# A fused convolution, attention and expert block: the first batch's side work dealt out anew over VectorE, GpSimd and TensorE

## The chip, the core and the metric

The kernel runs on one core of a Trainium2 chip. The metric is the device time in microseconds of one execution. All arrays are float32; the whole input, four images of 96 channels and 56 x 56 pixels, is worked through in one launch.

## The reference

What is computed, cut to what matters (x is (4, 96, 56, 56)):

```
xn    = layernorm over channels of x                       # eps 1e-6
value = depthwise 3x3 conv(xn, w_v) + b_v                  # stride 1
query = depthwise 3x3 conv(xn, w_q) + b_q                  # stride 1
key   = depthwise 3x3 conv(xn, w_k) + b_k                  # stride 2, 28 x 28
off   = depthwise 3x3 conv(xn, w_off1) + b_off1            # stride 2, 28 x 28
o     = gelu(layernorm over channels of off * ln_g + ln_b)
pos   = tanh(o @ w_off2 + reference points)                # (y, x) of each of 784 samples
vs    = bilinear sample of value at pos                    # four rows of value a sample
attn  = (query^T key) * 32^-0.5                            # 12 heads, 32 channels; no softmax
x     = x + w_out @ (attn vs)
t     = layernorm over channels of x, a row a pixel
gates = softmax(t @ gate_w + gate_b), the best 2 of 4 kept and renormalised
out   = x + sum over 4 experts of gate * (gelu(t @ w1 + b1) @ w2 + b2)
```

As there is no softmax in the attention, the kernel forms key times sampled values first, folds w_out into it, and applies the result to the query.

## The kernel before

Each engine runs its own instruction list in order; semaphores join them. The work goes batch by batch. The experts' matmuls of a batch (84 chunks of 448 pixels and 128 hidden units) are laid between the attention steps of the next batch by tables of numbers, which the change does not touch. The first batch has no experts to be laid between, so its attention part stands alone in roughly the first 140 us. Only this part changes.

The three functions head, first_rest and those that they call, on each engine, are the first batch:

- The image arrives in three DMAs. TensorE turns it into rows of pixels in seven slots, ScalarE evicts them, VectorE takes the statistics (L1098, then small instructions L1075 to L1088). The scaling is shared: VectorE scales the first tiles (L1114), ScalarE the last ones (L846). TensorE turns the image back into 128 partitions (a quarter of the image's rows by 32 channels, three blocks), and ScalarE writes it into a padded image xpad (L873), on which all four convolutions work. TensorE runs idle matmuls (spin, L607) where it would stand.
- The value and query convolutions of blocks 0 and 1 run on TensorE as nine accumulating matmuls with diagonal weights on half a block (convolve, L580); the diagonals are built by GpSimd (L1503). Block 2 of each, and the offset and key convolutions (stride 2, three blocks) run on VectorE, nine taps a block (tap, L1146 and L1149).
- offc: the normalised offsets are transposed on TensorE, ScalarE applies gelu (L896), TensorE multiplies by w_off2 (offsets, L601), VectorE adds the reference points (raw_positions, L1188), ScalarE applies tanh (L900), VectorE works out row numbers and weights (positions, to L1214).
- The values are transposed to rows of pixels in seven slots (valT, L631, L925), and SP writes them to a table in memory by four DMAs (L480): two after the fourth slot, two after the seventh. GpSimd gathers from the table by the row numbers, 16 indirect DMAs, two a tile (L1485), after both the row numbers and all four writes are there. VectorE weights them (sample, L1351 and L1354).
- key_values (L642), the head mask (L1364) and mixes (L652) follow, then attended (L672), the products with the query.

The PSUM tiles pa and pd are each used in turn by a list of jobs (act_jobs for ScalarE's evictions, dve_jobs for VectorE's); a job waits for the one two places ahead of it. The float32 expert weights are split into a high and a low part before the experts: w1 lies in the query's memory until then, so nothing may be written to query before weights_split. Names: KEYS_AHEAD key taps stand ahead of the positions; VALUE_HALF is the slot at which the first two table writes are issued; py, ph are PSUM tiles of TensorE's products.

## Time and profile before

| | us |
|---|---|
| median of 3 runs (748.31 to 748.81) | 748.49 |
| the profiled execution | 748.6 |
| its span, from the first instruction to the last | 746.8 |
| TensorE busy | 715.4 (96%) |
| VectorE busy | 583.9 (78%) |
| ScalarE busy | 384.6 (51%) |
| GpSimd busy | 213.0 (29%) |

Busy time is a sum over the whole span, and a busy TensorE is not TensorE at its peak: a float32 matmul has two records, and the granted clock (0.978 of 2.4 GHz in the mean) enters their length. For a change at one place the start and end of single instructions there say more. In the rows below a line's first number is the start in us from the span's start, the second the length in us; "x24" is the number of instructions merged; a bracket gives how long the engine stood before it and what ended that.

### The profile page before, as it was taken

The page shows a single profiled execution, that of the slowest core. Times are in us where ns is not written, and L with a number is a line of the kernel's source. Part 1 is how long each engine was busy: PE and PEld are TensorE (multiplying, and loading weights), DVE is VectorE, ACT ScalarE, POOL GpSimd, SP SyncE. Part 2 cuts the span into 40 slices and gives each one's busy share as a digit, 9 for nine tenths or more (in the row PEclk, how much of TensorE's full clock was granted, in tenths as well). Part 3 has the DMA queues.
Part 4 walks back from the last instruction along what each step waited for, and adds up shares of the span by engine and source line. Part 5 has one row for each costly group of instructions (what it writes and reads, how often), then busy time and mean ns, then how long its engine had stood idle before and what let it go on. Part 6 is the DMA issues. An engine that isn't in the chain of part 4 may idle for free.

```text
span 746.8 us, 9679 instructions
## 1 busy us (share of the span) xinstructions
PE 715.4 (96%) x3216; PEld 495.4 (66%) x3216; DVE 583.9 (78%) x1512; ACT 384.6 (51%) x722; POOL 213.0 (29%) x184
## 2 busy tenths in 40 slices
PE   7898999999999999899999999999989999999996
PEld 5556666566676666566766665666656665888884
DVE  6889558999999768799998577999955275677774
ACT  2313124754554525644646238545423256899995
POOL 4002700012138500111177101211375121344443
PEclk9798999999999999999999999999989999999998
DMA  8007200134464411354744403444545201121111
GB/s 199 6 0 203 57 1 1 40 74 92 95 187 114 107 30 14 73 128 93 195 105 113 70 11 58 83 102 91 165 103 111 32 28 41 47 74 47 66 47 37
DMA packets 29697, 58.66 MB, mean 79 GB/s; under 512 B 6224, under 2 KB 20176, under 8 KB 29360
## 3 DMA queue, kind: packets, MB, share of 16 engines
q0 software_dynamic: 11584, 17.90, 15.4%
q1 hardware_dynamic: 14336, 32.59, 14.3%
q10 hardware_dynamic: 3728, 7.55, 3.2%
q8 instruction: 26, 0.43, 0.3%
q14 instruction: 23, 0.19, 0.1%
HBM read 30.30 MB, written 14.65 MB: 60 GB/s over the span
## 4 chain that ended last, share of the span: by engine, by line
PE 81%; ACT 5%; DMA 4%; DVE 4%; POOL 2%; issue 2%; POOLq 0%; ACTq 0%; DVEq 0%
PE py L759 20%; PE pd L672 8%; PE ph L580 7%; PE ph L775 5%; PE ph L776 5%; PE ph L777 5%; PE pa L531 3%; PE pa L660 3%; PE pd L642 2%; PE ph L797 2%; PE ph L799 2%; PE ph L798 2%; PE py L809 2%; PE py L812 2%; PE py L810 2%
## 5 line engine op out<-in xcount | busy, mean ns | idle before, releaser
L759 PE MATMUL py<-hid,w 128*96 128x448 f32 x504 | 233.6, 544 | 8.0 <-ACT hid L1021 7.2
L1021 ACT ACTIVATE hid<-ph,b 128x448 f32<-128x448 f32 x252 | 158.9, 632 | 150.8 <-PE ph L777 147.3
L775 PE MATMUL ph<-x_hi,w_hi 96*128 96x448 f32 x252 | 164.6, 653 | 0.0
L1496 POOL DMA_DIRECT2D xbuf<-ye x76 | 64.3, 846 | 331.0 <-DMA xbuf<-ye 159.7
L1485 POOL DMA_INDIRECT big<-value_table,rows x64 | 86.2, 1348 | 88.3 <-DVE rows L1209 54.4
L759 PEld LDWEIGHTS py<-hid,w 128*96 128x96 f32 x504 | 81.3, 164 | 27.7 <-ACT hid L1021 11.8
L776 PE MATMUL ph<-x_lo,w_hi 96*128 96x448 f32 x252 | 93.2, 370 | 0.0
L777 PE MATMUL ph<-x_hi,w_lo 96*128 96x448 f32 x252 | 92.4, 367 | 0.0
L1432 DVE SCALAR_TENSOR_TENSOR ye<-py,b,gate_all 96x448 f32<-96x448 f32 x112 | 75.3, 675 | 11.5 <-PE py L759 7.9
L1498 POOL TENSOR_TENSOR xbuf<-xbuf,ye 96x448 f32<-96x448 f32 x36 | 53.9, 1498 | 102.5 <-DVE ye L1432 99.8
L1459 DVE TENSOR_TENSOR hid_lo<-hid,hid_hi 128x448 fp32r<-128x448 f32 x84 | 59.7, 711 | 27.2 <-ACT hid L1030 27.0
L1149 DVE SCALAR_TENSOR_TENSOR query<-xpad,conv_w,query 128x784 f32<-128x784 f32 x80 | 78.3, 1027 | 0.5
L1149 DVE SCALAR_TENSOR_TENSOR val<-xpad,conv_w,val 128x784 f32<-128x784 f32 x80 | 78.3, 1026 | 0.4
L775 PEld LDWEIGHTS ph<-x_hi,w_hi 96*128 96x128 f32 x252 | 48.0, 190 | 41.1 <-issue 40.7
L776 PEld LDWEIGHTS ph<-x_lo,w_hi 96*128 96x128 f32 x252 | 48.7, 193 | 35.9 <-issue 35.5
L672 PE MATMUL pd<-query,mix_area 128*96 128x392 f32 x192 | 67.2, 492 | 0.0
L1030 ACT ACTIVATE hid_hi<-ph,b 128x448 fp32r<-128x448 f32 x84 | 53.3, 634 | 6.9 <-PE ph L799 1.7
L1030 ACT ACTIVATE hid<-ph,b 128x448 f32<-128x448 f32 x84 | 52.5, 625 | 0.0
L841 ACT ACTIVATE big<-pa 112x400 f32<-112x400 f32 x28 | 14.0, 502 | 70.6 <-PE pa L660 70.6
L777 PEld LDWEIGHTS ph<-x_hi,w_lo 96*128 96x128 f32 x252 | 47.8, 190 | 3.5
L672 PEld LDWEIGHTS pd<-query,mix_area 128*96 128x96 f32 x192 | 29.5, 163 | 24.0 <-issue 24.0
L1370 DVE TENSOR_TENSOR xbuf<-pd,xbuf 96x392 f32<-96x392 f32 x32 | 17.9, 561 | 32.7 <-PE pd L672 32.5
(168 smaller groups left out, 1092.2 us busy)
## 6 DMA issues: line engine op xcount, KB each, us to landing
gate_all<-gate_rows SPq DMA_DIRECT2D x56, 336.0 KB, 3.4
xbuf<-ye POOLq DMA_DIRECT2D x76, 168.0 KB, 3.5
value_table<-valT ACTq DMA_DIRECT2D x6, 1176.0 KB, 8.5
out<-xbuf SPq DMA_DIRECT2D x28, 168.0 KB, 2.0
xbuf<-in_x SPq DMA_DIRECT2D x3, 1176.0 KB, 10.6
value_table<-valT SPq DMA_DIRECT2D x2, 672.0 KB, 5.4
big<-value_table,rows POOLq DMA_INDIRECT x64, 2.8
value_table<-valT SPq DMA_DIRECT2D x2, 504.0 KB, 5.0
```

The costliest lines, as they stand in the source:

```text
L672: last = nc.tensor.matmul(bank[0:C, 0:YPIX], mix[:, q, i, :], query[:, i, h * YPIX:(h + 1) * YPIX], start=(i == 0), stop=(i == BLOCKS - 1))
L759: nc.tensor.matmul(py[e % 2][0:C, 0:GPIX], w2[:, c, :], hid[:, k % 3, :], start=(j == 0), stop=(j == CPE - 1)).then_inc(hid_used, 1)
L775: nc.tensor.matmul(bank, w1_hi[:, cols], xh(b, g), start=True, stop=False)
L776: nc.tensor.matmul(bank, w1_hi[:, cols], xl(b, g), start=False, stop=False)
L777: nc.tensor.matmul(bank, w1_lo[:, cols], xh(b, g), start=False, stop=True).then_inc(hid_full, 1)
L1021: nc.scalar.activation(hid[:, k % 3, :], ph[k % 2][:, 0:GPIX], ACT.Gelu, bias=b1[:, k % NCH:k % NCH + 1]).then_inc(hid_act, 1)
L1030: nc.scalar.activation(dst[:, k % 3, :], ph[k % 2][:, 0:GPIX], ACT.Gelu, bias=b1[:, k % NCH:k % NCH + 1]).then_inc(ready, 1)
L1149: ins = v.scalar_tensor_tensor(to, src, w, to, ALU.mult, ALU.add)
L1432: v.scalar_tensor_tensor(ye[0:C, e, :], py[e % 2][0:C, 0:GPIX], b2[:, e:e + 1], gate_all[0:C, e, :], ALU.add, ALU.mult).then_inc(ye_ready, 1)
L1459: v.tensor_tensor(hid_lo[:, m % 2, :], hid[:, k % 3, :], hid_hi[:, k % 3, :].bitcast(f32), ALU.subtract).then_inc(hid_lo_ready, 1)
L1485: p.indirect_dma_start(got[:, tile, r, :, :].rearrange("p a c -> p (a c)"), None, table, bass.IndirectOffsetOnAxis(ap=rows[:, r, tile:tile ...
L1496: pool.dma_start(to, ye[0:C, e, :], accum_op=ALU.add).then_inc(ye_summed, 16)
```

## The change

All of it concerns the first batch.

- GpSimd, idle between the diagonals and the gathers, gets the upper half (392 of 784 elements a partition) of value block 2: one tensor_scalar, then eight times a tensor_scalar into a scratch half and a tensor_tensor that adds it. Behind it come the splits of w1 and w2, which stood on VectorE ahead of the offset taps. TensorE waits for the half block (value_low) ahead of the value transposes.
- VectorE does the lower half of value block 2 (half_tap, nine taps of 392), and takes over one of TensorE's eight half-block convolutions, the lower half of query block 1, in nine such taps behind the keys. Each tap waits for the one before.
- The offset norm and its transposes and gelu come ahead of all value transposes; the offset products stand behind four value slots (seven before), the tanh on ScalarE behind six. Three key taps instead of nine stand ahead of the raw positions, one more ahead of the tanh's result, five behind.
- TensorE transposes the offset tiles behind its second value convolution instead of its third. The gate-mean product moves between the first two, with the wait for the constants.
- VectorE scales five tiles instead of four and ScalarE two slots instead of three. TensorE spins twice instead of three times at the start and eight times instead of five behind the first transposes.

TensorE's list from the first convolution to the key-value products, before. L580 are convolutions, nine matmuls each; L568 transposes of offset (kv_area) and key tiles; L631 value slots, three matmuls each; L513 the transposes of normalised offsets; L601 the offset products; L531 the second batch's slots.

```order
16 L580 MATMUL ph<-xpad,xbuf 128x392 x27
17 L568 MATMUL pa<-ident,kv_area 98x128 x6
18 L580 MATMUL ph<-xpad,xbuf 128x392 x9
19 L623 MATMUL py<-gate_w,hid 96x4
20 L631 MATMUL pa<-ident,val 112x128 x12
21 L513 MATMUL pa<-ident,kv_area 96x98 x8
22 L631 MATMUL pa<-ident,val 112x128 x9
23 L601 MATMUL pd<-woff,mix_area 98x2 x8
24 L531 MATMUL pa<-ident_gate,xbuf 112x96 x8
25 L580 MATMUL ph<-xpad,gate_all 128x392 x18
26 L568 MATMUL pa<-ident,key_area 98x128 x6
27 L580 MATMUL ph<-xpad,ye 128x392 x18
```

The same place of TensorE's list now; the lines are L596, L584, L651, L529, L619 and L547 in the changed file.

```order
16 L596 MATMUL ph<-xpad,xbuf 128x392 x9
17 L639 MATMUL py<-gate_w,hid 96x4
18 L596 MATMUL ph<-xpad,xbuf 128x392 x9
19 L584 MATMUL pa<-ident,kv_area 98x128 x6
20 L596 MATMUL ph<-xpad,xbuf 128x392 x18
21 L529 MATMUL pa<-ident,kv_area 96x98 x8
22 L651 MATMUL pa<-ident,val 112x128 x12
23 L619 MATMUL pd<-woff,mix_area 98x2 x8
24 L651 MATMUL pa<-ident,val 112x128 x9
25 L547 MATMUL pa<-ident_gate,xbuf 112x96 x8
26 L596 MATMUL ph<-xpad,gate_all 128x392 x18
27 L584 MATMUL pa<-ident,key_area 98x128 x6
```

The offset transposes, which wait for the offset taps, now have two convolutions ahead of them and two behind. The transposes of the normalised offsets are ahead of every value slot, and the last query convolution is one instead of two.

VectorE's list from the scaling to the norm, before. kv_area holds the offsets, val the values.

```order
26 L1114 TENSOR_TENSOR xT<-xT,rstd 112x384 x3
27 L1227 CAST w_hi<-query 96x1536
28 L1228 TENSOR_TENSOR w_lo<-query,w_hi 96x1536
29 L1449 CAST w_hi<-w 128x1152
30 L1451 TENSOR_TENSOR w_lo<-w,w_hi 128x1152
31 L1146 TENSOR_SCALAR kv_area<-xpad,conv_w,conv_b 128x196 x3
32 L1149 SCALAR_TENSOR_TENSOR kv_area<-xpad,conv_w,kv_area 128x196 x24
33 L1146 TENSOR_SCALAR val<-xpad,conv_w,conv_b 128x784
34 L1149 SCALAR_TENSOR_TENSOR val<-xpad,conv_w,val 128x784 x8
35 L1176 BN_STATS st<-kv_area 98x6 x8
```

The same place of VectorE's list now.

```order
26 L1135 TENSOR_TENSOR xT<-xT,rstd 112x384 x4
27 L1167 TENSOR_SCALAR kv_area<-xpad,conv_w,conv_b 128x196 x3
28 L1170 SCALAR_TENSOR_TENSOR kv_area<-xpad,conv_w,kv_area 128x196 x24
29 L1185 TENSOR_SCALAR val<-xpad,conv_w,conv_b 128x392
30 L1188 SCALAR_TENSOR_TENSOR val<-xpad,conv_w,val 128x392 x8
31 L1213 BN_STATS st<-kv_area 98x6 x8
```

The four instructions of the splits are gone from it and the value taps have half their width.

The diff, without the declarations of the new semaphores and without three places where the numbers of scaled tiles are written as functions of the batch (scaled_by_dve and slots_scaled: FIRST_SCALED tiles in the first batch, TOP_TILES + 1 = 4 in the others):

```diff
--- before
+++ after
@@ -68,7 +68,7 @@
 
 def act_jobs():
 
-    order = jobs(0, "xT", NG) + jobs(0, "pad", 2 * BLOCKS) + jobs(0, "offT", 2) + jobs(0, "valT", QT)[:VALUE_HALF] + jobs(0, "offc", 2) + jobs(0, "valT", QT)[VALUE_HALF:]
+    order = jobs(0, "xT", NG) + jobs(0, "pad", 2 * BLOCKS) + jobs(0, "offT", 2) + jobs(0, "offc", 2) + jobs(0, "valT", QT)
     order += jobs(1, "xT", NG)[:EARLY_SLOTS] + jobs(0, "keyT", 2) + jobs(1, "xT", NG)[EARLY_SLOTS:] + jobs(0, "mix", QUARTERS) + jobs(0, "x1T", NG) + jobs(1, "pad", 2 * BLOCKS)
     order += jobs(0, "gateT", 1) + jobs(1, "offT", 2) + jobs(1, "offc", 2)
     for b in range(1, BATCH):
...
@@ -111,7 +111,10 @@
 
 QUERY_AHEAD = 2
 VALUE_AHEAD = 2
-KEYS_AHEAD = 9
+KEYS_AHEAD, KEYS_TO_TANH = 3, 4
+HALF = QH // 2
+FIRST_SCALED = 5
+OFFSETS_BEHIND, LIMIT_BEHIND = 4, 6
 SCALE_AFTER = 4
 FIRST_SPLITS, GATES_AFTER = 2, 3
 
...
@@ -398,7 +414,7 @@
             return dve_job(b, name, g)[1]
 
 
-        first_convs = [(m, i, h) for m in (VALUE, QUERY) for i in range(2) for h in range(2)]
+        first_convs = [(VALUE, 0, 0), (VALUE, 0, 1), (VALUE, 1, 0), (VALUE, 1, 1), (QUERY, 0, 0), (QUERY, 0, 1), (QUERY, 1, 0)]
         VALUE_CONVS = 4
 
         def dve_blocks(b):
...
@@ -608,19 +626,21 @@
 
             def head(b):
                 pe.wait_ge(zeros_ready, 1)
-                spin(3)
+                spin(2)
                 pe.wait_ge(tiles_zero, 1)
                 x_to_tokens(b)
-                spin(5)
+                spin(8)
                 quarters_back(b)
                 pe.wait_ge(act_done, acted(b, "pad", 2 * BLOCKS - 1))
                 pe.wait_ge(diag_ready, 2)
-                convolve(3)
+                pe.wait_ge(consts_in, NCONST)
+                pe.wait_ge(mean_filled, 1)
+                convolve(1)
+                nc.tensor.matmul(py[0][0:C, 0:EXPERTS], mean_of, gate_w[:, :], start=True, stop=True).then_inc(gate_mean, 1)
+                convolve(1)
                 to_samples(b, "offT", off, off_conv, 1)
-                convolve(1)
-                pe.wait_ge(mean_filled, 1)
-                pe.wait_ge(consts_in, NCONST)
-                nc.tensor.matmul(py[0][0:C, 0:EXPERTS], mean_of, gate_w[:, :], start=True, stop=True).then_inc(gate_mean, 1)
+                convolve(2)
+                off_to_channels(b)
 
             def values_to_tokens(b, before=lambda s: None, slots=range(QT)):
                 for s in slots:
...
@@ -706,19 +726,20 @@
 
             def first_rest(b, plan, chunks_to):
                 pe.wait_ge(conv_done, VALUE_CONVS)
-                values_to_tokens(b, slots=range(VALUE_HALF))
-                off_to_channels(b)
-                values_to_tokens(b, slots=range(VALUE_HALF, QT))
+                pe.wait_ge(value_low, 1)
+                values_to_tokens(b, slots=range(OFFSETS_BEHIND))
                 offsets(b)
+                values_to_tokens(b, slots=range(OFFSETS_BEHIND, QT))
                 x_to_tokens(b + 1, slots=range(EARLY_SLOTS))
                 pe.wait_ge(diag_ready, 4)
                 convolve(2)
                 to_samples(b, "keyT", key, key_conv, b + 1)
-                convolve(2)
+                convolve(1)
                 x_to_tokens(b + 1, slots=range(EARLY_SLOTS, QT))
                 key_values(b, range(QUARTERS))
                 mixes(b)
                 pe.wait_ge(conv_done, len(first_convs))
+                pe.wait_ge(query_low, 1)
                 pe.wait_ge(gate_centred, 1)
                 attended(b)
                 quarters_back(b + 1)
...
@@ -913,9 +934,11 @@
                 scaled(b)
                 padded(b)
                 act.wait_ge(conv_in, 32)
-                convolved(0, 3)
+                convolved(0, 2)
                 off_to_samples(b)
-                convolved(3, 4)
+                convolved(2, 4)
+                act.wait_ge(consts_in, NCONST)
+                off_gelu(b)
 
             def values_to_tokens(b, before=lambda s: None, slots=range(QT)):
                 for s in slots:
...
@@ -965,16 +988,14 @@
                 limit_positions(b)
 
             def first_rest(b, plan, gelus_to):
-                values_to_tokens(b, slots=range(VALUE_HALF))
-                act.wait_ge(consts_in, NCONST)
-                off_gelu(b)
-                values_to_tokens(b, slots=range(VALUE_HALF, QT))
+                values_to_tokens(b, slots=range(LIMIT_BEHIND))
                 limit_positions(b)
+                values_to_tokens(b, slots=range(LIMIT_BEHIND, QT))
                 x_to_tokens(b + 1, slots=range(EARLY_SLOTS))
                 act.wait_ge(weights_split, 1)
                 convolved(4, 6)
                 key_to_samples(b)
-                convolved(6, 8)
+                convolved(6, 7)
                 x_to_tokens(b + 1, slots=range(EARLY_SLOTS, QT))
                 mixes(b)
                 act.wait_ge(dve_done, dved(b, "kv", QUARTERS - 1))
...
@@ -1109,10 +1130,10 @@
 
             def scale_x(b):
                 by = x_stats_of(b).rstd[0:TP, :].rearrange("p (s o j u) -> p s o j u", j=QUARTERS, o=1, u=1)
-                for s in range(TOP_TILES + 1):
+                for s in range(scaled_by_dve(b)):
                     part = tiles_of(s)
                     ins = v.tensor_tensor(part, part, by[:, s, :, :, :].to_broadcast([TP, BLOCKS, QUARTERS, CB]), ALU.mult)
-                    if s >= TOP_TILES - 1:
+                    if s in (TOP_TILES - 1, scaled_by_dve(b) - 1):
                         ins.then_inc(x_normed, 1)
 
             def norm_x(b, turn):
...
@@ -1154,6 +1175,22 @@
 
             tapped = {}
 
+            def half_tap(m, i, k, dst, ready):
+
+                dy, dx = k // 3 + HALF, k % 3
+                src = xpad[:, i, dy:dy + HALF, dx:dx + W]
+                to = dst[:, i, HALF * W:].rearrange("c (h w) -> c h w", w=W)
+                w = conv_w[:, m, i, k:k + 1]
+                if k == 0:
+                    ins = v.tensor_scalar(to, src, w, conv_b[:, m, i:i + 1], ALU.mult, ALU.add)
+                else:
+                    need(tapped[(m, i)])
+                    ins = v.scalar_tensor_tensor(to, src, w, to, ALU.mult, ALU.add)
+                if k < TAPS - 1:
+                    tapped[(m, i)] = step(ins)
+                else:
+                    ins.then_inc(ready, 1)
+
             def off_tap(k):
                 tap(OFF, k, off, 2, off_conv, range(BLOCKS))
 
...
@@ -1223,16 +1260,12 @@
             def head(b):
 
                 norm_x(b, no_turn)
-                dve.wait_ge(consts_in, NCONST)
-                link(v.tensor_copy(w1_hi[:, :], w1))
-                v.tensor_tensor(w1_lo[:, :], w1, w1_hi[:, :].bitcast(f32), ALU.subtract).then_inc(weights_split, 1)
-                split_w2()
                 dve.wait_ge(conv_in, 32)
                 dve.wait_ge(act_done, acted(b, "pad", 2 * BLOCKS - 1))
                 for k in range(TAPS):
                     off_tap(k)
                 for k in range(TAPS):
-                    value_tap(b, k)
+                    half_tap(VALUE, 2, k, val, val_conv)
                 normalise_off(b, no_turn)
                 dve.wait_ge(gate_mean, 1)
                 v.tensor_tensor(ident_gate[:, C:XC], gate_w[:, :], py[0][0:C, 0:EXPERTS], ALU.subtract).then_inc(gate_centred, 1)
...
@@ -1241,9 +1274,14 @@
                 for k in range(KEYS_AHEAD):
                     key_tap(k)
                 raw_positions(b, no_turn)
+                for k in range(KEYS_AHEAD, KEYS_TO_TANH):
+                    key_tap(k)
                 positions(b, no_turn)
-                for k in range(KEYS_AHEAD, TAPS):
+                for k in range(KEYS_TO_TANH, TAPS):
                     key_tap(k)
+                dve.wait_ge(weights_split, 1)
+                for k in range(TAPS):
+                    half_tap(QUERY, 1, k, query, query_low)
                 for k in range(TAPS):
                     query_tap(b, k)
                 sample(b, no_turn)
...
@@ -1443,13 +1481,6 @@
 
                 return turn
 
-            def split_w2():
-
-
-                v.tensor_copy(w2_hi[:, :, :], w2[:, :, :]).then_inc(w2_part, 1)
-                dve.wait_ge(w2_part, 1)
-                v.tensor_tensor(w2_lo[:, :, :], w2[:, :, :], w2_hi[:, :, :].bitcast(f32), ALU.subtract).then_inc(w2_split, 1)
-
             def last_experts(outputs_to):
 
                 for k in range(EARLY_CHUNKS, ALL_CHUNKS):
...
@@ -1502,6 +1533,27 @@
             for m, i in ((VALUE, 0), (VALUE, 1), (QUERY, 0), (QUERY, 1)):
                 p.tensor_tensor(diag_of[(m, i)], ident[:, :].rearrange("c (o d) -> c o d", o=1).to_broadcast([128, TAPS, 128]),
                                 conv_w[:, m, i, :].rearrange("c (k o) -> c k o", o=1).to_broadcast([128, TAPS, 128]), ALU.mult).then_inc(diag_ready, 1)
+            pool.wait_ge(act_done, acted(0, "pad", 2 * BLOCKS - 1))
+            top = val[:, 2, 0:HALF * W].rearrange("c (h w) -> c h w", w=W)
+            parts = xbuf[2][:, 2 * TAPS * 128:2 * (TAPS * 128 + HALF * W)].rearrange("c (n p) -> c n p", n=2)
+            for k in range(TAPS):
+                src, w = xpad[:, 2, k // 3:k // 3 + HALF, k % 3:k % 3 + W], conv_w[:, VALUE, 2, k:k + 1]
+                if k == 0:
+                    ins = p.tensor_scalar(top, src, w, conv_b[:, VALUE, 2:3], ALU.mult, ALU.add)
+                else:
+                    part = parts[:, k % 2, :]
+                    p.tensor_scalar(part.rearrange("c (h w) -> c h w", w=W), src, w, None, ALU.mult).then_inc(value_part, 1)
+                    pool.wait_ge(value_part, k)
+                    pool.wait_ge(value_step, k)
+                    ins = p.tensor_tensor(val[:, 2, 0:HALF * W], val[:, 2, 0:HALF * W], part, ALU.add)
+                ins.then_inc(value_low if k == TAPS - 1 else value_step, 1)
+            pool.wait_ge(consts_in, NCONST)
+            p.tensor_copy(w1_hi[:, :], w1).then_inc(w1_part, 1)
+            pool.wait_ge(w1_part, 1)
+            p.tensor_tensor(w1_lo[:, :], w1, w1_hi[:, :].bitcast(f32), ALU.subtract).then_inc(weights_split, 1)
+            p.tensor_copy(w2_hi[:, :, :], w2[:, :, :]).then_inc(w2_part, 1)
+            pool.wait_ge(w2_part, 1)
+            p.tensor_tensor(w2_lo[:, :, :], w2[:, :, :], w2_hi[:, :, :].bitcast(f32), ALU.subtract).then_inc(w2_split, 1)
             pool.wait_ge(table_edge, 32)
             added = 0
             for b in range(BATCH):
```

## Rows read from the trace of the kernel before

**Rows 1.** Chain of waits, first 140 us: start, length, engine, tile, line, records
```profile
27.46 19.96 PE ph L580 x54
...
60.45 0.56 PE pa L631 x3
...
61.69 2.03 PE pd L601 x16
...
80.47 11.86 PE ph L580 x36
...
96.31 5.16 PE pd L642 x16
...
104.26 5.93 PE pd L672 x18
```

**Rows 2.** VectorE's timeline, first batch: start, length, engine, line, operation, shapes, number
```profile
28.86 8.96 DVE L1149 SCALAR_TENSOR_TENSOR kv_area<-xpad,conv_w,kv_area 128x196 f32<-128x196 f32 x24
...
38.46 8.53 DVE L1149 SCALAR_TENSOR_TENSOR val<-xpad,conv_w,val 128x784 f32<-128x784 f32 x8
48.46 1.38 DVE L1176 BATCH_NORM_STATS2 st<-kv_area 98x6 f32<-98x96 f32 x8 [1.47 <-ACT kv_area L881]
...
54.93 0.14 DVE L1238 TENSOR_TENSOR ident_gate<-gate_w,py 96x4 f32<-96x4 f32 x1
...
65.80 0.17 DVE L1198 TENSOR_SCALAR pos<-pt 98x16 f32<-98x16 f32 x1 [0.28 <-ACT pt L900]
...
68.64 0.16 DVE L1209 TENSOR_SCALAR rows<-ix 98x8 int32<-98x8 f32 x1
...
70.07 8.57 DVE L1149 SCALAR_TENSOR_TENSOR query<-xpad,conv_w,query 128x784 f32<-128x784 f32 x8
...
94.11 1.46 DVE L1354 SCALAR_TENSOR_TENSOR key_area<-big,w,key_area 98x96 f32<-98x96 f32 x6
```

**Rows 3.** GpSimd's timeline, gathers of the first batch
```profile
69.74 1.37 POOL L1485 DMA_INDIRECT big<-value_table,rows  x1 [54.45 <-DVE rows L1209]
71.41 1.64 POOL L1485 DMA_INDIRECT big<-value_table,rows  x1 [0.30 <-issue]
...
91.38 0.96 POOL L1485 DMA_INDIRECT big<-value_table,rows  x1 [0.30 <-issue]
```

**Rows 4.** Busy time by stretch: PE, PEld, DVE, ACT, POOL, clock, DMA, GB/s
```profile
22.00:31.00 9.00, 8.06 (x29) 6.30 (x30) 6.54 (x12) 2.87 (x6) 0.00 (x0) 0.50 0.01 3
```

**Rows 5.** ScalarE's timeline: gelu, last value slot, paddings of the second batch
```profile
57.78 1.28 ACT L896 ACT_TABLE_LOAD   x1 [0.36 <-PE pa L513]
59.07 1.24 ACT L896 ACTIVATE mix_area<-pa,ln_gb 96x392 f32<-96x392 f32 x2
...
61.72 0.49 ACT L925 ACTIVATE valT<-pa 112x384 f32<-112x384 f32 x1 [0.18 <-PE pa L631]
...
127.02 0.92 ACT L873 ACTIVATE xpad<-pa 128x392 f32<-128x392 f32 x2 [0.56 <-PE pa L558]
...
129.71 1.25 ACT L873 ACTIVATE xpad<-pa 128x504 f32<-128x504 f32 x2 [0.22 <-PE pa L536]
```

**Rows 6.** Timelines of GpSimd and VectorE near 14 and 610 us
```profile
13.19 2.10 POOL L1503 TENSOR_TENSOR ye<-ident,conv_w 128x1152 f32<-128x1152 f32 x1
...
14.55 0.81 DVE L1075 TENSOR_TENSOR sd<-st 112x28 f32<-112x28 f32 x1
...
604.79 1.13 POOL L1498 TENSOR_TENSOR xbuf<-xbuf,ye 96x448 f32<-96x448 f32 x1 [15.75 <-DVE ye L1432]
610.09 2.65 POOL L1498 TENSOR_TENSOR xbuf<-xbuf,ye 96x448 f32<-96x448 f32 x1 [4.17 <-DVE ye L1432]
...
611.67 1.21 DVE L1376 TENSOR_TENSOR sc<-big,rstd 112x112 f32<-112x112 f32 x1
```

**Rows 7.** Table writes of the first batch: issue and time to landing
```profile
L480 SPq DMA_DIRECT2D value_table<-valT x4: 304/406/631, 57.4 to 62.6; - x4
...
DMA to landing us min/median/max: 4.4/5.0/6.3
```

21 lines of the change are left out of this document (16 added, 5 removed).

## The prediction

> **What bounds the kernel now.** I read the chain that ended last first. In the first 140 us its long pieces are TensorE's [rows 1], so I looked for the place where the changed stretch, the first batch, hands over to the rest: the first attention products, which start at 104.26 us. Behind them the program is the same in both kernels, so whatever moves that moment moves the end by about as much.
>
> Two lines of work meet ahead of it, and the reader should follow both. One is TensorE: eight convolutions, 5.93 us each where it runs at full speed (36 records, two a matmul, in 11.86 us), then the key-value products from 96.31 [rows 1]. The other is the positions: the offset convolution on VectorE, its norm (done when VectorE goes on at 54.93), transposes, gelu, offset products, positions (row numbers at 68.8), sixteen gathers on GpSimd from 69.74 to 92.34, and sampling until 95.57 [rows 2, 3]. The two reach the key-value products within 0.8 us of each other. So taking a convolution off TensorE alone gives at most 0.8 us, and any delay of the positions beyond 0.8 us goes into the time in full. The change must be judged by when the gathers start.
>
> **The start.** ScalarE scales 8 pieces instead of 12, VectorE 5 tiles instead of 4. Eight spinning matmuls instead of 5 fill most of TensorE's pause before the padding transposes. In the kernel before the granted clock falls behind that pause: it is 0.50 (1.2 GHz) from 22 to 31 us [rows 4]. I assume that it holds now (2.4 GHz). Then the scaled image is padded at about 20.7 + 3.9 = 24.7, the 3.9 being the same six evictions of the second batch at full clock (127.02 to 130.96) [rows 5], against 27.4 before, where the first offset taps start 1.3 us ahead of 28.86 [rows 2]. The weight splits that leave VectorE cost nothing there before: they lay in its wait for the padding. Gain of this part: 2.7 us.
>
> **What VectorE does by its own durations.** Offset taps 10.2 us (3 and 24 pieces). Half a value block: nine taps of 392, between 0.37 (196 elements) and 1.07 us (784), by a straight line 0.61, so 5.6 instead of 9.2. Norm 6.5 (48.46 to 54.93) [rows 2]. Alone, the norm would end at 24.7 + 10.2 + 5.6 + 6.5 = 47.0, 8 us before its old 54.9.
>
> **What GpSimd adds, and the port.** GpSimd was idle from 15.3 to 69.7. Now it has 21 instructions from 24.7 on: 9 products of one tensor by a pointer (392 elements), 8 additions of two, two casts and two subtractions (1536 and 1152). Two-input ones have rows: 448 elements 1.13 us undisturbed, 1152 elements 2.10 [rows 6]. The straight line through them gives 1.05 for 392 and 2.63 for 1536. One-input ones have no row. They cost between nothing (if they keep nobody waiting) and the two-input price; I take 0.6, 1.6 and 1.3, a little over half of it, since they read half as much. Sum: 8 x 1.05 + 9 x 0.6 + 1.6 + 2.63 + 1.3 + 2.10 = 21.4 us; bounds 13 and 27.
>
> These do not lie beside VectorE's work, and that is the core of my forecast. At 14.55 a VectorE tensor_tensor of 28 elements, which has two inputs in SBUF, took 0.81 us, where small VectorE instructions take 0.16 or 0.17 [rows 2]; it ended 0.07 us behind the GpSimd instruction that ran from 13.19 to 15.29. At 610.09 a GpSimd addition took 2.65 us instead of 1.13: it waited for two VectorE instructions, and the next VectorE one, started at 611.67, took 1.21 and ended 0.14 us behind it [rows 6]. Each excludes the other while it runs. Every tap of VectorE (scalar_tensor_tensor: padded image and accumulator) has two inputs in SBUF.
>
> So each GpSimd instruction takes its time out of VectorE's, less what VectorE can hide of its fixed part, about 0.2 us (196 elements last 0.37, 784 last 1.07, so some 0.14 to 0.2 is not data). 21.4 - 21 x 0.2 = 17.2 us. All of it falls ahead of the end of the norm, since 17 + 22 us is longer than GpSimd's whole list. The norm ends at 47.0 + 17.2 = 64.2. Bounds: 47.0 (no exclusion) and 47.0 + 27 - 2 = 72.
>
> The Trainium skill, "SBUF — State Buffer", section "SBUF: two separate sides", calls this shared pair an exclusive lock held for the whole instruction. By full durations the loss would be 21.4 and the norm's end 68.4; that is 4 us more than my term. For the one-input products the "GPSIMD Engine Reference", section "Elementwise — side-by-side cycle accounting", has 1.03 cycles an element at most two operations; 392 elements would be an estimated 0.34 us and a dispatch, and my sum some 1 us less. No row here shows it.
>
> **TensorE in that stretch.** The offset tiles are transposed behind two convolutions now, ready at 24.7 + 11.9 = 36.6, but the offset taps end late: 17 GpSimd instructions (13.8 - 3.4 = 10.4) and the first two splits (3.8) fall among them, so 24.7 + 10.2 + 14.2 = 49. TensorE stands 12 us, with a lower clock behind it: the first three convolutions of the kernel before began at the low clock and took 19.96 instead of 17.8, so 2.2 [rows 1]. Its other two convolutions end at 49 + 0.7 + 11.9 + 2.2 = 63.8, just when the norm does.
>
> **From the norm to the gathers.** Transposes and gelu with its table load 3.1 (from the first transpose, 0.6 ahead of 57.78, to 60.31) [rows 5]; four value slots 2.2 (0.56 each on TensorE); offset products 2.0 [rows 1]; raw positions 0.4; one key tap 1.1 (three pieces of the 24 in 8.96 us), beside which the two value slots in front of the tanh are evicted (0.5 more); tanh to row numbers 3.0 (65.80 to 68.80) [rows 2]. 64.2 + 3.1 + 2.2 + 2.0 + 0.4 + 1.1 + 0.5 + 3.0 = 76.5. The last value slot follows the tanh's at about 74.2; its two table writes, issued in some 0.4 to 0.6 us each, take 5.0 more [rows 7]: 80.2. In the kernel before that landing (61.72 + 0.49 + 6 = 68.2) came ahead of the row numbers; now it is what the gathers wait for. They start at 80.2 instead of 69.7: +10.5.
>
> **To the hand-over.** Sixteen gathers take 22.6. One issued beside VectorE's query taps took up to 1.64 us, one late in the row 0.96 [rows 3]; VectorE has 20.6 us of taps beside them now (5 key, half a query block, a query block) instead of 9.3, which I put at 1.7. Last gather 104.5, sampled 3.2 later (92.34 to 95.57), 107.7. TensorE has done its three convolutions and token transposes at 98 and waits. The first two quarters of products are done; two remain, 2.6 of the 5.16 us [rows 1], behind a masking (0.6), then the mixes 2.8: 113.7. Before: 104.26. That is +9.4, and TensorE is cold after its wait, another 2.2 at most; I take 1.6. **Sum: +11.0 us** on the profiled execution's 748.6 (its span 746.8), which is 0.1 above the median of the runs, so 759.5.
>
> **Rivals.**
> *The work hides as meant* (chance 0.15). If strided taps and GpSimd products share the port, the norm ends at 47.0; TensorE's four convolutions end at 49.1; gelu at 52.3, last value slot 58, table 64, gathers 64 to 88.3, sampled 91.5, hand-over 96.9 to 99: 5 to 7 us gained, 742.5. For it: the norm really has 8 us of slack gained. Against: every two-input row that I found beside GpSimd shows the wait. It decides once the loss is under 5 us: table landing and longer tail need the norm by about 52.
> *VectorE keeps the port* (0.08). At 610.09 GpSimd was passed over once by a queued instruction. Passed over throughout the offset and value taps, it would begin its list near 41 and hold the value half block until 57. TensorE's value slots stand behind that wait and the offset products behind them; table at 68.5, hand-over 102 to 105: 746 to 749.
> *Half a loss* (0.15): 8 to 10 us instead of 17, since GpSimd waits between its own dependent steps. Then 750 to 755.
> *GpSimd at its upper price* (0.07): loss 23 to 25, about 767; if it still held its list past 80, the gathers would queue behind the splits too.
>
> **How the numbers follow.** Main case 0.55, 756 to 764. Faster by over 0.2%: 0.16 (first rival and a little of the second); within 0.2%, about what a measurement of this kernel can tell from no change: 0.05; slower: 0.79. The range leaves out most of the first rival and the far end of the last: 744 to 768; the main case alone has 754 to 765.
>
> **What would show it.** Right: the 27 offset taps take over 20 us; GpSimd additions of 1.05 us show up as 1.3 and more; the norm ends behind 60; TensorE stands before the offset transposes; the first gather waits for the table and starts behind 76. Wrong: offset taps done in 10 to 11 us and a first gather ahead of 69. If the clock falls in the padding after all, 2 us are to be added.

## The result, and the profile after

| | before | after |
|---|---|---|
| median (range, executions) | 748.4 us (746.95 to 748.81, 4) | 759.1 us (755.83 to 764.28, 4) |
| the profiled execution, its span | 748.6, 746.8 | 755.8, 754.0 |
| hand-over (first attention products) | 104.09 | 112.57 |
| TensorE, VectorE, GpSimd busy | 715.4, 583.9, 213.0 | 712.7, 594.8, 248.1 |

The changed kernel takes 1.0153 times as long (95% interval 1.0092 to 1.0214); forecast were 759.5 us and "slower". The profiled execution is the fastest of its four: in it the hand-over comes 8.5 us later and the end 7.2, against 11.0 forecast. (In the timeline the hand-over of the kernel before stands at 104.09, in the chain of rows 1 at 104.26; below I use the timeline's for all kernels.) GpSimd's busy time grew by 35 us; its 21 new instructions are 30.1 of them (24 to 76 us), and that already holds waiting. The medians below are of all executions of a kernel, while the ratios leave out those more than 1.5% above its fastest, among them e11's profiled one.

GpSimd's timeline of the changed kernel, which answers to its silence until 69.74 in [rows 3]:

```profile
24.48 0.66 POOL L1542 TENSOR_SCALAR val<-xpad,conv_w,conv_b 128x392 f32<-128x392 f32 x1 [9.57 <-ACT xpad L894]
25.13 1.27 POOL L1545 TENSOR_SCALAR xbuf<-xpad,conv_w 128x392 f32<-128x392 f32 x1
26.48 1.25 POOL L1548 TENSOR_TENSOR val<-val,xbuf 128x392 f32<-128x392 f32 x1
27.71 1.37 POOL L1545 TENSOR_SCALAR xbuf<-xpad,conv_w 128x392 f32<-128x392 f32 x1
29.16 1.11 POOL L1548 TENSOR_TENSOR val<-val,xbuf 128x392 f32<-128x392 f32 x1
...
45.58 1.79 POOL L1551 CAST w_hi<-query 96x1536 fp32r<-96x1536 f32 x1
47.46 3.63 POOL L1553 TENSOR_TENSOR w_lo<-query,w_hi 96x1536 fp32r<-96x1536 f32 x1
...
52.60 2.82 POOL L1556 TENSOR_TENSOR w_lo<-w,w_hi 128x1152 fp32r<-128x1152 f32 x1
78.42 1.21 POOL L1516 DMA_INDIRECT big<-value_table,rows  x1 [23.00 <-DMA value_table<-valT]
...
100.10 1.43 POOL L1516 DMA_INDIRECT big<-value_table,rows  x1 [0.30 <-issue]
```

Its VectorE, answering to [rows 2]. The last row is the same form as the second, later, with GpSimd only gathering:

```profile
25.76 14.81 DVE L1170 SCALAR_TENSOR_TENSOR kv_area<-xpad,conv_w,kv_area 128x196 f32<-128x196 f32 x24
...
41.20 11.73 DVE L1188 SCALAR_TENSOR_TENSOR val<-xpad,conv_w,val 128x392 f32<-128x392 f32 x8
52.86 1.36 DVE L1213 BATCH_NORM_STATS2 st<-kv_area 98x6 f32<-98x96 f32 x8
54.26 1.19 DVE L1095 TENSOR_TENSOR sa<-st 98x8 f32<-98x8 f32 x1
...
60.34 0.14 DVE L1271 TENSOR_TENSOR ident_gate<-gate_w,py 96x4 f32<-96x4 f32 x1
...
80.96 5.26 DVE L1188 SCALAR_TENSOR_TENSOR query<-xpad,conv_w,query 128x392 f32<-128x392 f32 x8
```

The offset taps take 14.81 us where they took 8.96, though nothing on VectorE changed in them. The half value block takes 11.73, and the same nine-tap form 5.26 when GpSimd computes nothing. The small addition at 54.26, 1.19 us long, ends 0.03 us behind the last subtraction on GpSimd, which ends at 55.42; the eight BATCH_NORM_STATS2 before it, which have one input, lie beside the same subtraction and take 1.36 us, as without it (1.37 in e2). The norm is done at 60.34 instead of 54.93.

One period of the offset taps, tap by tap, beside the addition at 29.16 and the product behind it:

```profile
29.32 1.17 DVE L1170 SCALAR_TENSOR_TENSOR kv_area<-xpad,conv_w,kv_area 128x196 f32<-128x196 f32 x1
30.26 1.37 POOL L1545 TENSOR_SCALAR xbuf<-xpad,conv_w 128x392 f32<-128x392 f32 x1
30.42 0.74 DVE L1170 SCALAR_TENSOR_TENSOR kv_area<-xpad,conv_w,kv_area 128x196 f32<-128x196 f32 x1
31.20 0.42 DVE L1170 SCALAR_TENSOR_TENSOR kv_area<-xpad,conv_w,kv_area 128x196 f32<-128x196 f32 x1
31.54 0.41 DVE L1170 SCALAR_TENSOR_TENSOR kv_area<-xpad,conv_w,kv_area 128x196 f32<-128x196 f32 x1
```

An undisturbed tap has 0.42 and starts 0.37 behind the last (8.96 us for 24). So the addition costs VectorE about 0.7 us and the product about 0.35, and the product itself takes 1.37 where the first one, beside a one-input tap, took 0.66: each engine waits for the other.

The chain of waits of the changed kernel, answering to [rows 1] (start, length, engine, tile, line, records):

```profile
66.62 2.50 PE pd L619 x16
...
71.44 0.50 ACT valT L948
72.30 5.12 DMA value_table<-valT
...
105.47 4.48 PE pd L662 x8
109.95 2.78 PE pa L672 x24
112.73 5.93 PE pd L692 x18
```

Before, TensorE's convolutions were the chain at 80 us. Now it runs through the norm, the offset products and value slots, the value table (72.30 to 77.42), all gathers (78.42 on) and the sampling; TensorE waits for them. The row numbers were there at 74.2, so the table's landing releases the gathers, as forecast.

Busy time by stretch of the changed kernel (start:end, length, busy time of PE, PEld, DVE, ACT and POOL, then the granted clock, DMA share, GB/s):

```profile
58.00:76.00 18.00, 13.92 (x64) 11.77 (x65) 11.37 (x50) 7.04 (x13) 0.00 (x0) 0.51 0.43 127
...
105.00:118.00 13.00, 12.53 (x49) 7.62 (x50) 5.01 (x19) 1.64 (x4) 0.00 (x0) 0.87 0.00 0
```

From 58 to 76 us, behind TensorE's waits for the offset taps and the norm, the clock stands at its lower level (0.51); the value slots and offset products lie there. From 105 to 118, behind the wait for the samples, it is 0.87.

### The profile page after: what moved, and what is told of

The parts are those of the page before. It is cut to its first block, busy times and chain, and to the rows that moved or that the text cites. A ratio compares the mean times of both kernels' runs of the same rounds, so it can differ in the third digit from the quotient of the medians.

```text
span 754.0 us, 9684 instructions
## 1 busy us (share of the span) xinstructions
PE 712.7 (95%) x3202; PEld 493.2 (65%) x3202; DVE 594.8 (79%) x1518; ACT 383.5 (51%) x717; POOL 248.1 (33%) x205
## 4 chain that ended last, share of the span: by engine, by line
PE 60%; DMA 11%; DVE 10%; POOL 8%; ACT 5%; issue 5%; POOLq 0%; ACTq 0%; SPq 0%; DVEq 0%
PE py L780 15%; PE pd L692 8%; DMA xbuf<-ye 7%; POOL big L1516 6%; PE ph L796 4%; PE ph L797 4%; PE ph L798 4%; PE pa L680 3%; DVE kv_area L1170 3%; DMA value_table<-valT 2%; PE ph L818 2%; PE ph L820 2%; PE ph L819 2%; PE py L830 2%; PE py L833 2%
## 5 line engine op out<-in xcount | busy, mean ns | idle before, releaser
L780 PE MATMUL py<-hid,w 128*96 128x448 f32 x504 | 233.2, 544 | 10.3 <-ACT hid L1042 7.1
L1527 POOL DMA_DIRECT2D xbuf<-ye x76 | 68.1, 896 | 325.4 <-DVE ye L1470 156.0
L780 PEld LDWEIGHTS py<-hid,w 128*96 128x96 f32 x504 | 81.3, 164 | 30.0 <-ACT hid L1042 11.7
L1529 POOL TENSOR_TENSOR xbuf<-xbuf,ye 96x448 f32<-96x448 f32 x36 | 53.9, 1498 | 102.4 <-DVE ye L1470 99.7
L1170 DVE SCALAR_TENSOR_TENSOR query<-xpad,conv_w,query 128x784 f32<-128x784 f32 x80 | 78.4, 1028 | 0.5
L797 PEld LDWEIGHTS ph<-x_lo,w_hi 96*128 96x128 f32 x252 | 48.4, 192 | 35.3 <-issue 34.8
L1170 DVE SCALAR_TENSOR_TENSOR val<-xpad,conv_w,val 128x784 f32<-128x784 f32 x72 | 70.0, 1025 | 0.1
L1051 ACT ACTIVATE hid<-ph,b 128x448 f32<-128x448 f32 x84 | 52.5, 625 | 0.0
## 6 DMA issues: line engine op xcount, KB each, us to landing
xbuf<-in_x SPq DMA_DIRECT2D x3, 1176.0 KB, 10.4
```

Of the source, the lines that this page charges most:

```text
L780: nc.tensor.matmul(py[e % 2][0:C, 0:GPIX], w2[:, c, :], hid[:, k % 3, :], start=(j == 0), stop=(j == CPE - 1)).then_inc(hid_used, 1)
L797: nc.tensor.matmul(bank, w1_hi[:, cols], xl(b, g), start=False, stop=False)
L1051: nc.scalar.activation(dst[:, k % 3, :], ph[k % 2][:, 0:GPIX], ACT.Gelu, bias=b1[:, k % NCH:k % NCH + 1]).then_inc(ready, 1)
L1170: ins = v.scalar_tensor_tensor(to, src, w, to, ALU.mult, ALU.add)
L1527: pool.dma_start(to, ye[0:C, e, :], accum_op=ALU.add).then_inc(ye_summed, 16)
```

## The experiments

My theory: two-input work of GpSimd and VectorE excludes each other, VectorE's list grows by GpSimd's time, and the positions chain carries that into the hand-over one for one. Rivals: GpSimd does not disturb, and the delay is in the new order of TensorE's list; or it is memory traffic in general and not the reading. Each ratio is to the kernel before on the same chip (its medians beside e1 to e12: 747.9 and 748.6). Executions start unevenly: the first offset tap (T0) comes between 24.45 and 28.84 us in kernels that have the new start (e4 aside). Two sources show in the traces. In e5 and e9 TensorE's first transposes take 10.6 us instead of 6.5; in e2, e7, e8 and e11 the six padding evictions take 4.9 to 5.1 us instead of 4.0, with a granted clock of 0.50 to 0.61 in one stretch of 3 us there. So the table gives the stages from T0: the norm is done when VectorE goes on behind it, "gathers" is the start of the first, "hand-over" that of the first attention products. Each row's stages are of one execution.

| kernel | median (executions) | ratio to before, 95% | T0 | norm done | gathers | hand-over | span |
|---|---|---|---|---|---|---|---|
| before | 748.4 (4) | 1 | 27.52 | +27.4 | +42.2 | +76.6 | 746.8 |
| after | 759.1 (4) | 1.0153 | 24.48 | +35.9 | +53.9 | +88.1 | 754.0 |
| e1 after again | 761.85 (6) | 1.0167 (1.0120 to 1.0215) | 25.29 | +35.9 | +54.1 | +91.2 | 760.0 |
| e2 nothing on GpSimd | 751.94 (11) | 1.0032 (1.0001 to 1.0063) | 26.92 | +25.8 | +43.6 | +78.4 | 748.9 |
| e3 value half alone there | 757.8 (6) | 1.0126 (1.0094 to 1.0157) | 25.30 | +30.0 | +48.5 | +83.5 | 756.4 |
| e4 splits alone, early | 760.27 (7) | 1.0167 (1.0137 to 1.0198) | 34.39 | +25.8 | +43.6 | +77.7 | 752.3 |
| e5 writes, splits | 754.88 (7) | 1.0104 (1.0066 to 1.0142) | 28.33 | +28.5 | +47.3 | +82.1 | 751.1 |
| e6 after, kept warm | 755.95 (6) | 1.0138 (1.0091 to 1.0186) | 24.45 | +35.9 | +52.5 | +84.7 | 749.5 |
| e7 start alone | 744.46 (12) | 0.9947 (0.9916 to 0.9978) | 26.37 | +25.8 | +40.6 | +74.2 | 743.6 |
| e8 e2, kept warm | 746.68 (12) | 0.9989 (0.9961 to 1.0018) | 26.29 | +25.8 | +43.1 | +75.4 | 745.7 |
| e9 e2, old slots | 750.03 (12) | 1.0018 (0.9992 to 1.0043) | 28.84 | +25.8 | +40.6 | +76.4 | 754.6 |
| e10 e9, kept warm | 742.31 (8) | 0.9915 (0.9887 to 0.9943) | 24.56 | +25.8 | +40.1 | +72.7 | 736.0 |
| e11 splits alone | 757.15 (10) | 1.0093 (1.0056 to 1.0130) | 26.57 | +32.1 | +51.1 | +88.3 | 761.7 |
| e12 e7, kept warm | 746.69 (12) | 0.9981 (0.9953 to 1.0008) | 24.55 | +25.8 | +40.6 | +73.3 | 736.3 |

**e1, the changed kernel again.** No edit.

> The changed kernel once more, to see how much one execution of it differs from another. Port theory: the first batch does not differ (attention of the first batch starts near 112.6 us, 8.3 us behind the kernel before), so the executions that took 760 and 764 us lost their rest elsewhere, at a lower granted clock: 755 to 765 us. Rival (the port contention itself varies): the first batch's hand-over moves by several us between executions.

Six more executions: 755.69 to 764.44. In the profiled one VectorE's instructions up to the norm last as in the first profile (offset taps 14.82, value half 11.73); so the exclusion does not vary between these two. What differs is the clock behind the wait for the samples. Busy time by stretch and TensorE's timeline of e1 (columns as above; the hand-over is the last row):

```profile
105.00:118.00 13.00, 11.78 (x35) 8.27 (x36) 2.65 (x7) 1.64 (x4) 0.00 (x0) 0.52 0.00 0
```

```profile
106.22 5.41 PE L662 MATMUL pd<-keyT,key_area 98*96 98x384 f32 x8 [4.43 <-DVE kv_area L1402]
111.42 5.28 PE L672 MATMUL pa<-wout,kv_area 96*128 96x96 f32 x24
116.49 7.41 PE L692 MATMUL pd<-query,mix_area 128*96 128x392 f32 x18
```

The clock is 0.52 throughout 105 to 118, where the other execution had 0.87; the mixes take 5.28 instead of 2.95, the first attention products 7.41 instead of 6.09. The hand-over moves 3.1 us beyond the later T0, the end 6. So the new waits of TensorE have a price that differs by execution, and the kernel's median is not its first profile.

**e2, nothing on GpSimd.** The value half and the splits go back to VectorE; start, order and the moved convolution stay.

```diff
-                    half_tap(VALUE, 2, k, val, val_conv)
+                    value_tap(b, k)
-                pe.wait_ge(value_low, 1)
+                link(v.tensor_copy(w1_hi[:, :], w1))        # and the rest of the splits,
                 dve.wait_ge(conv_in, 32)                    # ahead of this wait again
-            top = val[:, 2, 0:HALF * W] ...                 # GpSimd: block and splits gone
```

> The changed kernel with both pieces of GpSimd's new work back on VectorE (all of value block 2, and the weight splits where they stood); the new order and the start are kept. Port theory: offset taps last 10.2 us again, the norm ends near 51.6, gathers start near 67, first attention near 100.5, so 4 us under the kernel before: 744 to 746 us. Rival (the new order itself is what costs): still 752 us or more.

The norm is done 25.8 us behind T0 instead of 35.9, and the hand-over is 7.2 us earlier (9.7 from T0); the ratios differ by 1.35%, some 10 us. That is GpSimd's share, against the rival. But the kernel is not faster than before: I had expected the hand-over at 100.5 and 744 to 746 us, it came at 105.33 and 751.94. Of the 4.8 us of that miss 2.4 are the later T0 (26.92 instead of 24.5); the rest, the gain that I gave the new order and the moved convolution, is not there. e8 to e10 take this up.

**e3, the splits back on VectorE** (value half alone on GpSimd), and **e11, the value half back** (splits alone on GpSimd, behind the padded image):

```diff
 e3
+                link(v.tensor_copy(w1_hi[:, :], w1))        # VectorE, ahead of the padding's wait
-            p.tensor_copy(w1_hi[:, :], w1).then_inc(w1_part, 1)    # and so on
 e11
-                    half_tap(VALUE, 2, k, val, val_conv)
+                    value_tap(b, k)
             pool.wait_ge(act_done, acted(0, "pad", 2 * BLOCKS - 1))
             p.tensor_copy(w1_hi[:, :], w1).then_inc(w1_part, 1)
```

> Only the weight splits go back to VectorE, the half value block stays on GpSimd. Port theory: GpSimd's list ends near 47, the offset taps still take 20 us less the end of it (14.8 as in the changed kernel, starting 1.1 us later behind the splits), half the value taps run free, the norm ends near 56; about 3 to 4 us less than the changed kernel in the first batch: 752 to 756 us. Rival (the splits cost nothing, being behind the value work): no gain.

> Only the weight splits on GpSimd, waiting for the padded image as in the changed kernel (e4 let them run at 14.7 us beside the statistics, and the padding came 10 us late). Port theory: four GpSimd instructions of 8 to 9.5 us fall beside the offset taps, which take 14 to 16 us instead of 8.96 in all; hand-over between e2's 105.3 and the changed kernel's 112.6, near 109: 753 to 756 us. Rival (a GpSimd list of few long instructions is harmless): offset taps near 10.

VectorE's timeline of e3, and VectorE's and GpSimd's of e11 (the row at 31.70 is one of the 24 taps, shown singly):

```profile
26.57 14.82 DVE L1170 SCALAR_TENSOR_TENSOR kv_area<-xpad,conv_w,kv_area 128x196 f32<-128x196 f32 x24
...
42.02 6.84 DVE L1188 SCALAR_TENSOR_TENSOR val<-xpad,conv_w,val 128x392 f32<-128x392 f32 x8
```

```profile
27.85 15.28 DVE L1169 SCALAR_TENSOR_TENSOR kv_area<-xpad,conv_w,kv_area 128x196 f32<-128x196 f32 x24
...
28.06 3.50 POOL L1539 TENSOR_TENSOR w_lo<-query,w_hi 96x1536 fp32r<-96x1536 f32 x1
31.51 1.27 POOL L1540 CAST w_hi<-w 128x1152 fp32r<-128x1152 f32 x1
31.70 1.30 DVE L1169 SCALAR_TENSOR_TENSOR kv_area<-xpad,conv_w,kv_area 128x196 f32<-128x196 f32 x1
32.86 2.62 POOL L1542 TENSOR_TENSOR w_lo<-w,w_hi 128x1152 fp32r<-128x1152 f32 x1
```

Either half of GpSimd's work stretches the same 24 taps from 8.96 us to about 15. A cast, which reads one tensor, holds a tap as the subtractions do (1.30 us at 31.70 instead of 0.42). Undisturbed, the norm is done at T0 + 25.8 with the whole value block on VectorE, and 3.3 us earlier (9.2 less 5.9) with half of it: 22.5, an estimate, since no kernel ran that. The value half on GpSimd costs 30.0 - 22.5 = 7.5 us, the splits 32.1 - 25.8 = 6.3, both together 35.9 - 22.5 = 13.4, nearly their sum. In e3, too, the gathers wait for the table (73.78, the row numbers at 66.4). e11's profile has the low clock behind the samples like e1's, so its hand-over says little. Both times were forecast too low (752 to 756 against 757.8, 753 to 756 against 757.15): e3's norm (55.25 against 56) and e11's taps (15.28 against 14 to 16) came as forecast, so what was forecast too low lies behind them. By the ratios e11 is 0.7% below the changed kernel's second set, and the intervals just touch.

**e4, the value half back, splits early.** Here the splits have no wait for the padded image.

```diff
-                    half_tap(VALUE, 2, k, val, val_conv)
+                    value_tap(b, k)
-            pool.wait_ge(act_done, acted(0, "pad", 2 * BLOCKS - 1))
```

> Only the half value block goes back to VectorE, the splits stay on GpSimd and run from 24.5 us beside the offset taps. Port theory: they take 7.6 to 9 us of the port, VectorE loses 5 to 7; the norm ends near 24.5 + 11.5 + 9.2 + 6.5 + 6 = 57 and the time is 749 to 753 us. Rival (only the long chain of small instructions hurts): offset taps as long as in the kernel before, norm near 51, 743 to 745 us.

I had expected the splits beside the taps; with the value half the edit also took away the wait for the padded image, so they ran at 14.68 to 23.5, beside the statistics. Timelines of GpSimd and VectorE of e4:

```profile
16.22 3.42 POOL L1538 TENSOR_TENSOR w_lo<-query,w_hi 96x1536 fp32r<-96x1536 f32 x1
16.24 3.45 DVE L1099 TENSOR_TENSOR sd<-sd 112x28 f32<-112x28 f32 x1
...
20.81 2.65 POOL L1541 TENSOR_TENSOR w_lo<-w,w_hi 128x1152 fp32r<-128x1152 f32 x1
21.02 2.47 DVE L1103 TENSOR_SCALAR si<-sv 112x28 int32<-112x28 int32 x1
23.53 0.18 DVE L1104 TENSOR_SCALAR rstd<-si 112x28 int32<-112x28 int32 x1
```

A VectorE instruction on 28 elements, 0.19 us elsewhere, takes 3.45 and ends 0.05 behind the GpSimd subtraction: the plainest picture of the exclusion. The scaling starts at 25.74 instead of 18.09 (7.7 us late), the padding evictions then take 5.7 us instead of 4.0, and T0 goes to 34.39, while the offset taps last 8.96 again. So 8.7 us of GpSimd work cost more ahead of the long chains than among them (6.3): the ratios, 1.0167 and e11's 1.0093, have intervals apart. The forecast of 749 to 753 us was for the other place, and this kernel does not test it; e11 does.

**e5, writes only.** GpSimd's products and additions become 17 memsets of 784 elements and one of 392; the upper half of value block 2 is left at zero. The splits stay.

```diff
-                    p.tensor_scalar(part.rearrange("c (h w) -> c h w", w=W), src, w, None, ALU.mult).then_inc(value_part, 1)
-                    ins = p.tensor_tensor(val[:, 2, 0:HALF * W], val[:, 2, 0:HALF * W], part, ALU.add)
+            for k in range(2 * TAPS - 1):
+                p.memset(wide, 0.0).then_inc(value_low if k == 2 * TAPS - 2 else value_step, 1)
```

> The changed kernel with GpSimd's 17 products and additions replaced by one clearing of the half block and 17 memsets of 784 elements into the scratch, each waiting for the one before: as many instructions, but none that reads SBUF. The upper half of value block 2 is left at zero. The weight splits stay on GpSimd. If what excludes is that both engines read two streams of SBUF (the port theory as I read the rows): the 24 offset taps take 8.96 us again instead of 14.81, the value taps up to the splits are free. Rival (any GpSimd instruction excludes VectorE, writes too, or the chip shares bandwidth): offset taps of 12 us or more.

Timelines of GpSimd and VectorE of e5:

```profile
28.75 13.71 POOL L1543 MEMSET xbuf<- 128x784 f32 x17
...
29.61 8.97 DVE L1170 SCALAR_TENSOR_TENSOR kv_area<-xpad,conv_w,kv_area 128x196 f32<-128x196 f32 x24
...
39.20 10.23 DVE L1188 SCALAR_TENSOR_TENSOR val<-xpad,conv_w,val 128x392 f32<-128x392 f32 x8
...
42.40 1.47 POOL L1547 CAST w_hi<-query 96x1536 fp32r<-96x1536 f32 x1
43.95 3.63 POOL L1549 TENSOR_TENSOR w_lo<-query,w_hi 96x1536 fp32r<-96x1536 f32 x1
```

Beside memsets the offset taps take their undisturbed 8.97; the value taps, which meet the splits, still take 10.23. So it is not traffic by writes, and not GpSimd being busy: memsets, which only write, do not hold VectorE's taps, while products, additions, casts and subtractions, which read, do. The Trainium skill, "SBUF — State Buffer", section "SBUF: two separate sides", says just this of VectorE operations with two SBUF inputs: locked "only against a GpSimd op that reads SBUF". Here e5 (8.97) beside e3 (14.82) agrees. This kernel's norm is 6.0 late (28.5 - 22.5), the splits' price again.

**e6, the changed kernel kept warm:** idle matmuls wherever TensorE would wait.

```diff
+                spin(5)
                 to_samples(b, "offT", off, off_conv, 1)
                 convolve(2)
+                spin(7)
                 off_to_channels(b)
+                spin(2)
...
-                key_values(b, range(QUARTERS))
+                key_values(b, range(2))
+                spin(5)
+                key_values(b, range(2, QUARTERS))
```

> The changed kernel with idle matmuls in TensorE's four new pauses: 5 before the offset transposes, 7 before the norm's, 2 behind them, 5 between the second and the third quarter of key-value products. If the low clock behind the pauses costs what I think (value slots 0.76 instead of 0.5, offset products 2.5 instead of 1.3, last two quarters 4.5 to 5.4 instead of 2.6, and in slow executions the mixes): gathers start about 3 us earlier, 5 to 8 us in all, 751 to 754 us, and the executions agree better. Rival (the spread comes from elsewhere, the pauses hide nothing): unchanged, 757 to 762.

The hand-over is 3.4 us earlier, the offset products take 1.47 instead of 2.71, and the mean clock is 0.992 instead of 0.978. The medians differ by 3 to 6 us from the two sets of the changed kernel, but the intervals of the ratios overlap, and the forecast (751 to 754) is missed by 2. Of the 11.7 us between T0 + 42.2 and T0 + 53.9 in the gathers' start only 1.4 go (52.5), of the 11.5 at the hand-over 3.4. The clock is the smaller part.

**e7, the start alone, in the kernel before.**

```diff
-                spin(3)
+                spin(2)
                 pe.wait_ge(tiles_zero, 1)
                 x_to_tokens(b)
-                spin(5)
+                spin(8)
-                for s in range(TOP_TILES + 1):
+                for s in range(scaled_by_dve(b)):           # five tiles in the first batch
```

> The kernel before with only the start of the change: two spins instead of three, eight instead of five, five scaled tiles on VectorE. If the clock holds, the padding is ready near 25 us and VectorE, whose splits end at 25.7, starts its offset taps 1.9 us earlier; everything behind moves by that: 746 to 747 us. Rival (the clock falls behind the pause all the same, or the DMA of the identity decides): no change, 748.

Faster, and by more than forecast: 0.9947 (0.9916 to 0.9978). The hand-over is at 100.61, 3.5 us earlier: 1.1 of it from T0, 1.6 because the norm no longer waits for evicted offset tiles (27.4 to 25.8; the three convolutions ahead of their transposes take 18.05 us instead of 19.96), and 0.7 behind the gathers, where TensorE's convolutions ended last before and start earlier now. It is the one part of the change that was tried in the kernel before, and it pays by itself.

**e8, e2 kept warm; e9, e2 with the old order of the value slots; e10, e9 kept warm.**

```diff
 e9: order of TensorE and ScalarE as before
-                off_to_channels(b)
                 ...
-                values_to_tokens(b, slots=range(OFFSETS_BEHIND))
-                offsets(b)
-                values_to_tokens(b, slots=range(OFFSETS_BEHIND, QT))
+                values_to_tokens(b, slots=range(VALUE_HALF))
+                off_to_channels(b)
+                values_to_tokens(b, slots=range(VALUE_HALF, QT))
+                offsets(b)
 e10, on top of e9
+                spin(2)                                      # behind off_to_channels
+                spin(5)                                      # between the halves of key_values
+                split_w2()                                   # behind the query taps
```

> The changed kernel with nothing new on GpSimd (as e2) and idle matmuls in the pauses: 2 before the norm's transposes, 2 behind, 6 between the second and third quarter. Clock theory: slots and offset products at the full clock bring the gathers from 70.6 to about 68, the last two quarters 2.6 instead of 5.4: hand-over near 100, 743 to 746 us. Rival (the new order costs by itself): 749 or more.

> As e2 (nothing new on GpSimd, one convolution on VectorE, the new start), but with the order of the kernel before: four value slots, the offset transposes and gelu, three value slots, the offset products, all nine key taps ahead of the positions. Table theory (e2 lost its head start because the table's 2.35 MB, 10 us of writing from the first issue, start behind the gelu): the first write goes out near 54, the row numbers release the gathers again near 67, hand-over 98 to 101 instead of 105.3: 743 to 746 us. Rival (e2's loss is the low clock alone): the first write moves, the hand-over stays at 104 or more.

> As e9, with the w2 split moved behind VectorE's query taps, two idle matmuls behind the offset transposes and five between the second and third quarter of key-value products, and one key tap moved behind the raw positions. Table and clock theory together: hand-over 97 to 99, 741 to 744 us. Rival (the gathers or their landing set it): as e9.

(e9 has nine key taps ahead of the raw positions like the kernel before, e10 eight and one.) e8 differs from e2 by idle matmuls alone: its hand-over is 3.0 us earlier from T0 (101.74, forecast near 100), its median 746.68, 0.7 above the forecast; the intervals of the two ratios overlap slightly. In e2 and e8 the gathers wait for the table (row numbers at 66.2 and 63.1, gathers at 70.56 and 69.42): the four writes, 2.35 MB, have landed 10.4 and 10.6 us behind the first issue, and the new order issues the first two only behind the gelu. With the old slots the gathers follow the row numbers again, 3.0 us earlier from T0 (e9). Yet e9's hand-over, forecast at 98 to 101, is at 105.28, and its time as e2's: its T0 is 1.9 us later, and TensorE's timeline shows the rest. e10's follows, with its first gather:

```profile
96.28 4.13 PE L661 MATMUL pd<-keyT,key_area 98*96 98x384 f32 x8 [2.65 <-DVE kv_area L1407]
...
100.21 5.27 PE L671 MATMUL pa<-wout,kv_area 96*128 96x96 f32 x24
```

```profile
64.68 1.20 POOL L1524 DMA_INDIRECT big<-value_table,rows  x1 [49.70 <-DVE rows L1248]
...
88.16 3.92 PE L625 MATMUL py<-hid 128*128 128x448 f32 x10
...
91.92 2.75 PE L661 MATMUL pd<-keyT,key_area 98*96 98x384 f32 x8
...
94.50 2.95 PE L671 MATMUL pa<-wout,kv_area 96*128 96x96 f32 x24
...
97.29 6.09 PE L691 MATMUL pd<-query,mix_area 128*96 128x392 f32 x18
```

The convolution moved to VectorE leaves TensorE 2.65 us of wait before the last key-value products. Behind it these take 4.13 instead of 2.75, the mixes 5.27 instead of 2.95 and the first attention products 7.36 instead of 6.09. With five idle matmuls in that place (88.16) everything behind it runs at full length: hand-over 97.29 and 742.31 us in the median, as forecast, 0.9915 (0.9887 to 0.9943) of the kernel before. It beats both kernels, and it uses GpSimd for nothing but its old work. e10 differs from e9 in three more things (two spins, a split and a key tap moved), so the idle matmuls' share of the 1% between them is read from these instructions and not from a kernel of its own. e10's gain at the end of the profiled execution (10.8 us) is larger than at the hand-over (6.8); the other 4 us come behind the third batch's hand-over (416.13 against 422.55 us), where the kernel before has stretches of lower clock (0.68 from 550 to 560 us, 0.83 from 620 to 630) that this execution has not. Why was not tried.

Put in a row, the hand-overs from T0 give the parts of the change, roughly, since each is from one execution and holds that one's stretches of low clock: 74.2 with the new start alone (e7), 76.4 with the convolution moved too (e9), 78.4 with the new order (e2), 88.1 with GpSimd's work (the changed kernel).

**e12, e7 kept warm** (w2 split behind the query taps, two idle matmuls behind the offset transposes).

```diff
-                split_w2()
...
+                split_w2()                                   # behind the query taps
+                spin(2)                                      # behind off_to_channels
```

> e7 (the kernel before with the new start) with the w2 split moved behind VectorE's query taps and two idle matmuls behind the offset transposes. VectorE is ready 2.1 us earlier for the padded image, but the image itself is ready at 26.3 in e7, so 0 to 1 us; the spins keep the clock for the value slots, the offset products (1.3 to 1.5 instead of 2.6) and the first token slots: 1 to 2 us. Together 742 to 744. Rival (the gathers' 22.6 us from the row numbers set it, and those do not move): 744.5 as e7.

The forecast of 742 to 744 is missed. The profiled execution is the fastest of its twelve (738.07), their median 746.69, not under e7's 744.46; the intervals overlap, so whether these two measures do anything is open. A single profile can lie 8.6 us from a median here. Against e10, measured beside it, e12 is slower, with intervals apart (0.9953 to 1.0008 and 0.9887 to 0.9943): the moved convolution, with its wait filled, is most of what sets them apart.

## Why the prediction was right, and where its terms were off

The forecast of the median, 759.5, met 759.1 partly by two errors that cancel, which is luck. Its mechanism held in each link: exclusion (e3, e4, e5, e11), norm late, table landing behind the row numbers, hand-over late by the same amount (from e2 to the changed kernel, from T0: norm 10.1, gathers 10.3, hand-over 9.7). Of its five signs of being right three came (norm behind 60, TensorE standing before the offset transposes, the first gather waiting for the table at 78.42). Two did not: the 27 offset taps took 16.1 us, not over 20, and the additions 1.0 to 1.25, not 1.3 and more. The sizes:

- **Start.** T0 24.5 against 24.7 forecast; full clock throughout. Right in that execution; by e7 the start is worth 3.5 at the hand-over (2.7 forecast). But T0 scatters by up to 4.4 us between kernels with this start, which I did not know, and the assumption that the clock holds through the padding failed in four of the profiled executions (e2, e7, e8, e11).
- **The port.** VectorE lost 13.4 us, not 17.2; norm done at 60.3, not 64.2. The term that was off is "each GpSimd instruction takes its time out of VectorE's, less ... about 0.2 us" in the value part: 7.5 instead of 13.8 - 3.4 = 10.4. Three of the nine products (24.48, 25.13 and 40.34) begin beside or just ahead of one-input instructions of VectorE, and neither these nor the taps behind them are longer; I had priced each at 0.4. An addition cost about 0.7 where I had 0.85, the other products about 0.35 where I had 0.4. The splits came out right (6.3 against 6.8 by the same rule) by luck: undisturbed they take 8.7 us in e4 and not 7.6, since a subtraction of 1536 has 3.42 and one of 1152 2.65 where my line through 448 and 1152 elements gave 2.63 and 2.10; and in e11 the first cast, 1.46, lies beside one-input taps and costs nothing. The loss lies between the main case and the rival "half a loss" (8 to 10 us).
- **TensorE's wait for the offset tiles.** Forecast ready at 49 and a wait of 12 us, but the timeline has them at 40.6 and TensorE standing for 3.9: I put all 17 value instructions and two splits in front, though only 13 of them lie ahead of 40.3 and the splits fall wholly into the value taps and the norm. Nothing hung on it but the clock.
- **Norm to gathers.** 18.1 us instead of 16.0. I took slots and offset products as the kernel before has them (0.56, 2.0); at a clock of 0.51 they took 0.76 and 2.5. I had foreseen the low clock only for the two convolutions.
- **Gathers to hand-over.** 34.3 us (78.42 to 112.73 in the chain) instead of 33.5 and 1.6 for the low clock, right in that execution.
- **Sum.** 8.5 instead of 11.0 in the profiled execution. The median is 3.3 us above that execution; the four, 755.8, 757.8, 760.4 and 764.3 us, have mean clocks of 0.978, 0.974, 0.972 and 0.965, and e1's trace shows such a longer stretch of low clock (0.52 for 13 us). That term is missing in the forecast: TensorE's wait for the samples does not only cost 1.6 us "cold", it costs about 2 (the last two quarters in the first profile) to 6 (quarters, mixes and attention products in e1), by execution.

My rival "the work hides as meant" failed by the exclusion, and its chain behind the norm was sound. It had 17 us from the norm to the gathers and 33 to 35 from there to the hand-over; e2, where GpSimd does nothing new, has 17.8 and 34.8. e2's hand-over of 105.3, less its later T0 (2.2) and the half value block that it still has on VectorE (3.3), gives an estimate of 99.8 for that rival, 1 to 3 us above its 96.9 to 99, and no run shows it.

## What to carry to other kernels

An idle GpSimd is not free time for a VectorE-bound stretch: GpSimd work that reads SBUF is taken out of VectorE's two-input chains in good part (13.4 us for 30.1 of GpSimd's busy time; 6.3 for 8.7 of the splits' own time), so reckon with a sum and not with the maximum. Here it relieved VectorE's chain of 3.3 us. When a convolution is taken off a nearly saturated TensorE, fill the wait that appears with idle matmuls before judging the move (e2 against e8, e9 against e10). And try the parts of a bundled change singly: one part of this one was worth 0.5%, in a whole that lost 1.5%.

## What the runs showed of the hardware

- The exclusion goes by reading on GpSimd's side: memsets of 784 elements, 17 in 13.71 us, left VectorE's two-input taps at 8.97 us; products, additions, casts and subtractions did not. The waits go both ways: a product took 1.37 us beside such taps and 0.66 beside a one-input one.
- In e4 a one-input VectorE instruction on 28 contiguous elements waited too (2.47 us beside the subtraction at 20.81), while in e11 three strided one-input taps beside a cast kept their 1.25 us, and in the changed kernel eight BATCH_NORM_STATS2 beside a subtraction their 1.36. Which one-input forms wait was not separated. The section of the skill named at e5 also has "a 2-port perf mode" among what takes the lock; whether the 28-element form ran in one no run shows.
- The changed kernel came out of TensorE's wait for the samples with a granted clock of 0.87 in the mean of 13 us once (wait 3.74 us) and of 0.52, the lower level, another time (4.43 us). The wait's length alone does not decide how long the clock stays low: behind 8.49 us in e3 the mixes took 2.95 us again, behind 2.65 us in e9 5.27.
- GpSimd is neither starved nor favoured beside a chain of taps: a product and an addition took 2.4 to 2.6 us a pair from start to start, from 27.71 to 42.78 us.
